# Window attention scores as one full-array product a tile, and routing selections over 128 rows, in a one-core transformer-and-Mamba kernel

## The chip, the cores and the metric

The kernel runs on one NeuronCore of a Trainium2 chip. The metric is the device time of one execution in microseconds (us). Engines are named as the profile names them: PE is TensorE (PEld its weight loads), DVE is VectorE, ACT is ScalarE, POOL is GpSimd, SP is SyncE, which here only issues DMAs. The profile gives the clock that was granted to TensorE as a share: 1.00 is 2.4 GHz, 0.50 is 1.2 GHz.

## The reference

The input is 4 images of 64 x 64 tokens with 64 channels. Three blocks follow one another:

```
xw = windows of 8 x 8 tokens; q, k, v = split(xw @ qkv_w.T + qkv_b), 8 heads of 8
q, k = rope2(q), rope2(k)
attn = softmax(q * hd**-0.5 @ k.T);  h = (attn @ v) @ proj_w.T + proj_b
...
h = h + mamba(layernorm(h))          # 128 inner channels, 16 states, a scan over 4096 tokens
...
logits = softmax(relu(f @ router_w1 + b1) @ router_w2 + b2)     # f = layernorm(h), 6 experts
top_w, top_i = top_k(logits, 2);  weights = softmax(top_w)
out = sum over the two chosen experts of weight * expert(f)     # three layers each
h = h + out
```

## The kernel before

The 16384 tokens are cut into 16 chunks of 1024 (16 image rows, so 16 attention windows). The stages are laid over one another: while chunk c is scanned, chunk c+1 is prepared (convolution, silu, softplus), c+2 is projected and normalised, c+3 is attended, and c-1 goes through router and experts. A round of the program (`body(c, odd)`, c from -3 to 17) has 32 slots, written out by hand: each engine has its own program with the same slots, and in each slot it does in a fixed order what falls due there. Engines run in order and are tied by semaphores. Score tiles belong to slots 18 to 25 of round c (`attention_at`, line 285, gives chunk c+3 and s = n - 9 from slot 9 on, and the rest of its steps in slots 0 to 8 of the next round).

**Scan.** For each slot, SP spreads rows of delta and x*delta from DRAM over 128 partitions (8 channels by 16 states), ACT makes the decay (L776), DVE multiplies by the spread B (L1015, "feed") and scans 512 tokens (L1024), POOL multiplies the result by the spread C (L1273), and PE collects four such products at every fourth slot (L439). ACT makes the decay of slot n+2 only after the scan of slot n. The B of a half chunk is spread by PE with L429: that for the first half of the next chunk in slot 30. POOL's product of slot n has to be there before DVE scans slot n+4.

**Attention.** Eight pairs of windows make a chunk. A tile w is one pair: 128 queries (64 of the upper window, 64 of the lower) against 8 heads by 64 keys. `q_diag` holds the queries of tile w as 128 x 128 with two filled quarters: the 64 channels of either window stand in their own 64 partitions and give 64 of the 128 output rows; the other two quarters are zero, from the setup on. For odd tiles the two halves of the output are swapped. `k_heads` holds the keys, zero outside the head's 8 channels. `scores` (L521) makes the scores of two tiles at once: two products of 64 rows by 64 columns for each, in the four quarters of the array, each over 512 columns, into banks 4 and 5 (a use's `fill` waits until the bank's use before was drained). They are only there for the maxima: DVE reduces each tile (L1044) to the negative maximum of every query and head, one tile a slot in slots 19 to 26. The eight results are transposed (L472), and `turned` makes the scores again in transposed form (L544), with the maxima added (L546), ACT takes the exponential (L795), and L559 multiplies by the values.

**Experts.** The routing weights of chunk c-1 (6 experts, a high and a low part in fp32r, for two groups of tokens: 24 rows) are computed by DVE in slots 15 to 19, transposed by PE in slot 22 (L646) into `wT`, and `weights` (L665) makes six products with `w_sel` in slots 23 to 28 (L673), each of which copies a weight over 64 output rows. One bank serves all six: each waits for ACT's copy of the one before (in slots 24 to 29). POOL multiplies the expert's second layer by it (L1345, slots 25 to 30) and `layer3` (L709; L714 in the profile) adds it up in slots 27, 29 and 31. The bias products L653 stand in slot 25. The first and second expert layers are L694 and L705 (slots 15 to 20), with ACT's activations L956 and L960.

PE's order within a slot is: B spread, first attention steps, late expert steps, y collection, C spread, expert steps, preparation, attention (score tiles among it), projection, expert layers, selections.

```
725    k, s = attention_at(c, n)
...
736    if has(c) and n % 4 == 1 and n >= 5:
737        collect(c, odd, (n - 5) // 4)
...
744    if has(k):
745        attend(k, s)
...
749        layers(c - 1, n, before_layers)
750        weights(c - 1, n, *before_weights)
```

Of the kernel before, what the change touches and what calls it, by code (L numbers as in the profile page):

```python
# [7 lines left out]
F32 = mybir.dt.float32  # L8
F32R = mybir.dt.float32r
# [12 lines left out]
NW = IMG // WIN  # L22
# [3 lines left out]
E, EP, RH = 6, 3, 32  # L26
# [38 lines left out]
for _w in range(NW):  # L65
# [17 lines left out]

AT = {"S": [9, 11, 13, 15], "max": [10 + _w for _w in range(NW)],
      "T": [19, 20, 22, 23, 25, 26, 28, 29], "P": [21, 21, 24, 24, 27, 27, 30, 30]}
# [30 lines left out]
def tower(nc, x, packed, select, out):  # L116
    with ExitStack() as ctx:
        def sb(name, shape, dt=F32):
            return ctx.enter_context(nc.sbuf_tensor(name, shape, dt))
# [17 lines left out]
        A = bank_uses("a", A_USES, 4)  # L137
# [10 lines left out]
        wts = sb("wts", [128, N_KEPT])  # L148
        w_sel = sb("w_sel", [4 * E, 2 * EP, 128], F32R)
        eps = sb("eps", [128, 6])  # L150
# [11 lines left out]
        q_diag = sb("q_diag", [128, NW, 128])  # L162
# [38 lines left out]
        fT = sb("fT", [128, 512])  # L201
        wT = sb("wT", [4 * E, 512], F32R)
        eb3_2 = sb("eb3_2", [4 * E, 2, C])
# [13 lines left out]
        def col(name, a=0, b=None):  # L217
            lo, hi = COL[name]
            lo2, hi2 = lo + a, hi if b is None else lo + b
            if lo >= N_KEPT:  # L220
                return once[:, lo2 - N_KEPT:hi2 - N_KEPT]
            return wts[:, lo2:hi2]
# [197 lines left out]
        def _(pe):  # L420
# [22 lines left out]
            def fill(use, k):  # L443
                if use.index or past(k - 1):
                    pe.wait_ge(use.drained, use.opens(k))
# [28 lines left out]
            def attend(k, s):  # L474
# [18 lines left out]
                if s in AT["S"]:  # L493
                    scores(k, 2 * AT["S"].index(s))
                for w in range(NW):
# [25 lines left out]
            def scores(k, w):  # L521

                uses = A[f"S{w}"], A[f"S{w + 1}"]
                for use in uses:
                    fill(use, k)
                if w == 0:
                    pe.wait_ge(heads_in.sem, heads_in.at(k, 192))
                    pe.wait_ge(heads_act.sem, heads_act.at(k, HEADS // 2))
                for odd, use in enumerate(uses):
                    for half in range(2):  # L530
                        p, to = slice(64 * half, 64 * half + 64), 64 * (half ^ odd)
                        last = pe.matmul(use.bank[to:to + 64, :], q_diag[p, w + odd, to:to + 64], k_heads[p, w + odd, :, :],  # L532
                                         start=True, stop=True)
                    last.then_inc(use.filled, 1)

# [74 lines left out]
            def experts(k, n):  # L610
# [38 lines left out]
                if n == 25:  # L649
                    use = F["outT"]  # L650
                    fill(use, k)
                    for s in range(2):
                        pe.matmul(use.bank[64 * s:64 * s + 64, :], eb3_2[:, s, :], wT[:, :].bitcast(F32),  # L653
                                  start=True, stop=True)
# [102 lines left out]
            pe.wait_ge(placed, 192)  # L757
            pe.wait_ge(setup_dve, 10)
            pe.wait_ge(setup_pool, 14)
# [4 lines left out]
        def _(act):  # L764
# [3 lines left out]
            def copy(out_, in_):  # L768
                return act.activation(out_, in_, ACT.Copy)  # L769
# [141 lines left out]
            def experts(k, n):  # L911
# [27 lines left out]
                if n == 22:  # L939
                    use = F["wT"]  # L940
                    act.wait_ge(use.filled, use.full(k))
                    copy(wT[:, :], use.bank[0:4 * E, :]).then_inc(use.drained, 1)
                if n == SLOTS:
# [60 lines left out]
            act.wait_ge(setup_pool, 14)  # L1004
            act.wait_ge(setup_dve, 10)
            rounds(body)

        @block.vector
        def _(dve):
# [181 lines left out]
            def body(c, odd):  # L1191
# [30 lines left out]
            dve.wait_ge(staged, 64)  # L1222
            dve.tensor_copy(w_sel[:, :, :], staging[0:4 * E, 0:2 * EP * 128].rearrange("p (a b) -> p a b", a=2 * EP))\
               .then_inc(setup_dve, 1)
            dve.tensor_copy(d_col[:, :], col("d_skip")).then_inc(setup_dve, 1)
            dve.tensor_scalar(conv_w[:, 0, :], col("conv_in"), col("normw"), None, ALU.mult).then_inc(setup_dve, 1)
            dve.tensor_scalar(z_w[:, :], col("z_in"), col("normw"), None, ALU.mult).then_inc(setup_dve, 1)
            dve.wait_ge(setup_dve, 6)
            dve.tensor_tensor(conv_w[:, 1, :], conv_w[:, 0, :], col("conv_tap", 128, 256), ALU.mult)\
               .then_inc(setup_dve, 1)  # L1230
            dve.wait_ge(setup_dve, 8)
            dve.tensor_tensor(conv_w[:, 0, :], conv_w[:, 0, :], col("conv_tap", 0, 128), ALU.mult)\
               .then_inc(setup_dve, 1)
            dve.wait_ge(setup_pe, 1)
            dve.tensor_copy(h_bias[:, :], b_ps[:, 0:C]).then_inc(setup_dve, 1)
            dve.wait_ge(setup_dve, 10)
            dve.wait_ge(setup_pool, 14)
# [3 lines left out]
        def _(pool):  # L1241
# [118 lines left out]

            pool.memset(staging[0:4 * E, :], 0.0).then_inc(setup_pool, 1)
            pool.memset(q_diag[:, :, :], 0.0).then_inc(setup_pool, 1)
# [11 lines left out]
            pool.wait_ge(setup_pool, 14)  # L1374
            pool.wait_ge(setup_dve, 10)
            rounds(body)
# [102 lines left out]
```

## Time and profile before

| | |
|---|---|
| time, three runs | 1921.57, 1922.06 (median), 1926.98 us |
| profiled execution | 1921.26 us |
| its span, first to last instruction | 1919.4 us |
| busy share of PE, DVE, POOL, ACT | 71%, 71%, 63%, 54% |
| mean granted TensorE clock | 0.74 |
| PE matmul records | 8212 |

An f32 matmul leaves two records in the profile, an fp32r one leaves one. A row of the profile names an instruction by its line, engine, operation and the tiles (out<-in); "64*64" behind it is the part of the array used, in rows and columns; in brackets is the idle time of the engine ahead of it and what ended it. Where rows are merged, "x8" counts the records. Records of products that share the array overlap, so a group's length is from its first start to its last end.

### The profile page before, as it was taken

The numbers are of one execution on the slowest core, as the hardware profiler recorded it, in microseconds if no ns is written. First come the engines' busy times: TensorE is split into PE (matmuls) and PEld (weight loads), VectorE is DVE, ScalarE is ACT, GpSimd is POOL, SyncE is SP. The second block draws the span as 40 slices with busy tenths as digits, with TensorE's granted clock in tenths as the row PEclk, the third lists the DMA queues.
The fourth block names the chain that finished last, engine by engine and source line by source line (L and its number), as shares of the span: only waits on it lengthen the run. The fifth ranks groups of instructions, "written<-read, shape, count | busy, mean of one in ns | idle before, by whom it ended". The sixth has DMA issues, their size and how long they took to land. (4 is left out here: it accounts for less than half of the span.)

```text
span 1919.4 us, 26560 instructions
## 1 busy us (share of the span) xinstructions
PE 1368.6 (71%) x8212; PEld 612.8 (32%) x8212; DVE 1353.5 (71%) x1834; ACT 1035.8 (54%) x1909; POOL 1207.9 (63%) x1666
## 2 busy tenths in 40 slices
PE   3675676776869687786968777685968777666565
PEld 1443242241515233141524324151524324121111
DVE  1114697778687877778697777868687777878941
ACT  2244556465655657465665646565655646554432
POOL 2205676667576766757676676757676675877651
PEclk9877777786877677686868778687867768576755
DMA  2005595657566564755666565765666575677820
GB/s 63 15 1 148 143 266 140 188 149 201 165 162 192 154 179 139 207 166 167 178 174 181 139 195 151 202 166 163 197 157 176 143 199 169 196 195 205 221 73 6
DMA packets 215205, 303.80 MB, mean 158 GB/s; under 512 B 79436, under 2 KB 79640, under 8 KB 214936
## 3 DMA queue, kind: packets, MB, share of 16 engines
q1 hardware_dynamic: 215064, 302.10, 57.1%
q8 instruction: 67, 1.10, 0.2%
q14 instruction: 74, 0.61, 0.1%
HBM read 274.75 MB, written 20.97 MB: 154 GB/s over the span
## 5 line engine op out<-in xcount | busy, mean ns | idle before, releaser
L1273 POOL TENSOR_TENSOR hc<-hs,c_rep 128x512 f32<-128x512 f32 x512 | 649.7, 1269 | 406.7 <-DVE hs L1024 406.4
L1024 DVE TENSOR_TENSOR_SCAN hs<-bank,state,xd 128x512 f32<-128x512 f32 x512 | 651.7, 1275 | 55.7 <-issue 49.3
L776 ACT ACTIVATE bank<-dl,a_neg 128x512 f32<-128x512 f32 x512 | 351.0, 687 | 371.7 <-DVE hs L1024 363.1
L1015 DVE TENSOR_TENSOR xd<-xd,bank 128x512 f32<-128x512 f32 x512 | 337.0, 663 | 101.1 <-PE bank L429 100.9
L544 PE MATMUL bank<-q_diag,k_heads 128*128 128x128 f32 x1024 | 206.1, 327 | 6.4 <-ACT top_row L769 4.9
L439 PE MATMUL bank<-hc,wts 128*32 128x512 f32 x1024 | 199.9, 843 | 5.9 <-POOL hc L1273 5.4
L544 PEld LDWEIGHTS bank<-q_diag,k_heads 128*128 128x128 f32 x1024 | 174.8, 212 | 73.3 <-issue 63.5
L705 PE MATMUL bank<-e,wts 64*64 64x512 f32 x384 | 84.2, 960 | 129.9 <-ACT e L956 129.9
L532 PE MATMUL bank<-k_heads,q_diag 64*64 64x512 f32 x512 | 92.2, 797 | 102.7 <-DVE neg_max L1044 70.6
L1044 DVE TENSOR_REDUCE neg_max<-bank 128x8 f32<-128x512 f32 x128 | 86.9, 687 | 103.8 <-PE bank L532 103.3
L1345 POOL TENSOR_TENSOR ew<-ew,e 128x512 f32<-128x512 f32 x96 | 121.0, 1261 | 33.5 <-ACT e L769 33.5
L1289 POOL TENSOR_TENSOR att<-pv,rec 128x512 f32<-128x512 f32 x16 | 17.2, 1074 | 191.5 <-DVE rec L1064 191.5
L602 PE MATMUL bank<-xz,wts 128*128 128x512 f32 x128 | 98.5, 862 | 46.9 <-ACT xz L870 41.8
L795 ACT ACTIVATE probsT<-bank 128x512 f32<-128x512 f32 x128 | 76.3, 596 | 100.1 <-PE bank L546 98.4
L1064 DVE RECIPROCAL rec<-pv 128x64 f32<-128x64 f32 x16 | 8.9, 554 | 158.7 <-ACT pv L769 158.7
L546 PE MATMUL bank<-top_row,top_sel 128*128 128x128 bf16 x512 | 119.3, 233 | 0.0
L694 PE MATMUL bank<-fT,wts 64*128 64x512 f32 x192 | 83.9, 962 | 49.1 <-ACT ew L960 46.1
L673 PE MATMUL bank<-wT,w_sel 24*128 24x512 f32 x96 | 70.8, 737 | 36.9 <-ACT e L769 33.9
L769 ACT ACTIVATE e<-bank 128x512 f32<-128x512 f32 x96 | 56.5, 589 | 52.3 <-PE bank L673 49.0
L714 PE MATMUL bank<-ew,wts 128*64 128x512 f32 x96 | 78.3, 912 | 3.8 <-POOL ew L1345 3.7
L559 PEld LDWEIGHTS bank<-v_diag,probsT 128*64 128x64 f32 x2048 | 67.3, 138 | 42.6 <-issue 36.3
L559 PE MATMUL bank<-v_diag,probsT 128*64 128x18 f32 x2048 | 75.3, 213 | 4.7 <-ACT probsT L795 4.7
(171 smaller groups left out, 2416.2 us busy)
## 6 DMA issues: line engine op xcount, KB each, us to landing
xd<-xdel_rows SPq DMA_DIRECT2D x512, 256.0 KB, 4.0
dl<-delta_rows SPq DMA_DIRECT2D x512, 256.0 KB, 3.7
delta_rows<-delta SPq DMA_DIRECT2D x16, 512.0 KB, 7.3
xdel_rows<-xdel SPq DMA_DIRECT2D x16, 512.0 KB, 4.0
xin<-in_x_dram SPq DMA_DIRECT2D x32, 128.0 KB, 2.5
q_diag<-rot SPq DMA_DIRECT2D x64, 64.0 KB
out_dram<-res SPq DMA_DIRECT2D x256, 16.0 KB
k_heads<-rot SPq DMA_DIRECT2D x128, 16.0 KB
```

Source lines behind the costliest of these rows:

```text
L439: last = pe.matmul(y_ps[32 * g:32 * g + 32, :], col("y_sel", 32 * i, 32 * i + 32), hc[:, n % 8, :], start=False, stop=True, skip_group_che ...
L532: last = pe.matmul(use.bank[to:to + 64, :], q_diag[p, w + odd, to:to + 64], k_heads[p, w + odd, :, :], start=True, stop=True)
L544: pe.matmul(use.bank[:, at], k_heads[:, w, 2 * hp:2 * hp + 2, :], q_diag[:, w, :], start=True, stop=True)
L546: last = pe.matmul(use.bank[:, at], top_sel[:, row:row + 2, :], top_row[:, :], start=False, stop=True, skip_group_check=True)
L559: last = pe.matmul(use.bank[64 * par:64 * par + 64, 18 * hp:18 * hp + 18], probsT[:, w % 2, 128 * hp + 64 * (par ^ w % 2):128 * hp + 64 * ...
L602: pe.matmul(use.bank[:, :], col(wt), xz[:, q, h, :], start=True, stop=True).then_inc(use.filled, 1)
L776: act.activation(decay_ps[n % 2][:, :], dl[:, n % 4, :], ACT.Exp, scale=a_neg[:, g:g + 1])\
L1015: dve.tensor_tensor(xd[:, n % 8, :], xd[:, n % 8, :], b_ps[:, :], ALU.mult).then_inc(injected.sem, 1)
L1024: dve.tensor_tensor_scan(hs[:, n % 4, :], decay_ps[n % 2][:, :], xd[:, n % 8, :], state[:, g:g + 1], ALU.mult, ALU.add).then_inc(scanned.s ...
L1044: dve.tensor_reduce(neg_max[:, w, :], use.bank[:, :].rearrange("p (h j) -> p h j", h=HEADS), X_AXIS, ALU.max, negate=True).then_inc(use.dr ...
L1273: pool.tensor_tensor(hc[:, n % 8, :], hs[:, n % 4, :], c_rep[:, BAND * h:BAND * h + BAND], ALU.mult)\
L1345: pool.tensor_tensor(ew[:, j, :], ew[:, j, :], wb[:, i % 2, :], ALU.mult).then_inc(weighed.sem, 1)
```

## The change

The score products are made tile by tile: `scores` makes one product of 128 x 128 over 512 columns for one tile, with the zero quarters of `q_diag` in it, and each of the eight tiles has a slot of its own (18 to 25 of the round) in place of two tiles in every other slot. The banks and the maxima's slots stay; tile w now waits for the bank's drain by tile w-2 only when its own slot comes. The selections L673 read `w_sel` and `wT` over all 128 rows: 24 filled ones and 104 of zeros, for which the staging tile and `wT` are cleared in the setup. One DVE operation is added there, and the counts of `setup_dve` that are waited for go up by one.

```diff
-AT = {"S": [9, 11, 13, 15], "max": [10 + _w for _w in range(NW)],
+AT = {"S": [9 + _w for _w in range(NW)], "max": [10 + _w for _w in range(NW)],
...
-        w_sel = sb("w_sel", [4 * E, 2 * EP, 128], F32R)
+        w_sel = sb("w_sel", [128, 2 * EP, 128], F32R)
...
-        wT = sb("wT", [4 * E, 512], F32R)
+        wT = sb("wT", [128, 512], F32R)
...
                 if s in AT["S"]:
-                    scores(k, 2 * AT["S"].index(s))
+                    scores(k, AT["S"].index(s))
...
             def scores(k, w):
 
-                uses = A[f"S{w}"], A[f"S{w + 1}"]
-                for use in uses:
-                    fill(use, k)
+                use = A[f"S{w}"]
+                fill(use, k)
                 if w == 0:
                     pe.wait_ge(heads_in.sem, heads_in.at(k, 192))
                     pe.wait_ge(heads_act.sem, heads_act.at(k, HEADS // 2))
-                for odd, use in enumerate(uses):
-                    for half in range(2):
-                        p, to = slice(64 * half, 64 * half + 64), 64 * (half ^ odd)
-                        last = pe.matmul(use.bank[to:to + 64, :], q_diag[p, w + odd, to:to + 64], k_heads[p, w + odd, :, :],
-                                         start=True, stop=True)
-                    last.then_inc(use.filled, 1)
+                pe.matmul(use.bank[:, :], q_diag[:, w, :], k_heads[:, w, :, :], start=True, stop=True)\
+                  .then_inc(use.filled, 1)
...
-                        pe.matmul(use.bank[64 * s:64 * s + 64, :], eb3_2[:, s, :], wT[:, :].bitcast(F32),
+                        pe.matmul(use.bank[64 * s:64 * s + 64, :], eb3_2[:, s, :], wT[0:4 * E, :].bitcast(F32),
                                   start=True, stop=True)
...
-                    copy(wT[:, :], use.bank[0:4 * E, :]).then_inc(use.drained, 1)
+                    copy(wT[0:4 * E, :], use.bank[0:4 * E, :]).then_inc(use.drained, 1)
...
-            dve.tensor_copy(w_sel[:, :, :], staging[0:4 * E, 0:2 * EP * 128].rearrange("p (a b) -> p a b", a=2 * EP))\
+            dve.tensor_copy(w_sel[:, :, :], staging[:, 0:2 * EP * 128].rearrange("p (a b) -> p a b", a=2 * EP))\
                .then_inc(setup_dve, 1)
+            dve.memset(wT[:, :].bitcast(F32), 0.0).then_inc(setup_dve, 1)
...
-            pool.memset(staging[0:4 * E, :], 0.0).then_inc(setup_pool, 1)
+            pool.memset(staging[:, :], 0.0).then_inc(setup_pool, 1)
```

## Rows read from the trace of the kernel before

**Rows 1.** The page: busy us of PE, its share of the span, its instructions.

```profile
PE 1368.6 (71%) x8212; PEld 612.8 (32%) x8212; DVE 1353.5 (71%) x1834; ACT 1035.8 (54%) x1909; POOL 1207.9 (63%) x1666
```

**Rows 2.** Stretches: us; busy us (instructions) of PE, PEld, DVE, ACT, POOL; clock, DMA, GB/s.

```profile
1037.50:1146.80 109.30, 83.06 (x515) 37.70 (x513) 84.74 (x115) 64.04 (x119) 75.06 (x103) 0.75 0.63 172
1108.48:1118.72 10.24, 6.39 (x29) 1.28 (x28) 8.47 (x13) 5.39 (x11) 5.85 (x11) 0.50 0.82 224
1125.54:1142.61 17.07, 15.40 (x46) 5.09 (x46) 12.75 (x15) 8.29 (x15) 16.11 (x20) 0.50 0.70 212
1142.61:1173.33 30.72, 28.26 (x288) 19.08 (x284) 20.73 (x25) 20.93 (x40) 16.97 (x24) 1.00 0.70 187
```

**Rows 3.** Waits of the whole span: us in total, times, longest us.

```profile
DVE neg_max L1044 <- PE bank L532: 103.3, 40, 13.4
...
PE bank L532 <- DVE neg_max L1044: 70.6, 34, 3.8
```

**Rows 4.** Timeline, DVE: start us, us, instruction, count, idle before and what ended it.

```profile
1112.61 0.69 DVE L1044 TENSOR_REDUCE neg_max<-bank 128x8 f32<-128x512 f32 x1 [0.39 <-PE bank L532]
...
1120.92 0.69 DVE L1044 TENSOR_REDUCE neg_max<-bank 128x8 f32<-128x512 f32 x1 [3.49 <-PE bank L532]
...
1145.61 1.29 DVE L1015 TENSOR_TENSOR xd<-xd,bank 128x512 f32<-128x512 f32 x2 [6.77 <-PE bank L429]
```

**Rows 5.** Timeline of PE, slots 20 to 22 of that chunk.

```profile
1110.60 1.99 PE L532 MATMUL bank<-k_heads,q_diag 64*64 64x512 f32 x8 [2.07 <-DVE neg_max L1044]
1114.36 1.99 PE L705 MATMUL bank<-e,wts 64*64 64x512 f32 x8 [1.78 <-ACT e L956]
1116.28 1.94 PE L439 MATMUL bank<-hc,wts 128*32 128x512 f32 x8
1118.14 0.87 PE L646 MATMUL bank<-wts,w_parts 128*24 128x128 f32 x4
1118.85 1.02 PE L602 MATMUL bank<-xz,wts 128*128 128x512 f32 x2
1119.80 1.09 PE L532 MATMUL bank<-k_heads,q_diag 64*64 64x512 f32 x8
```

**Rows 6.** Timeline of PE, slots 25 to 31 of that chunk.

```profile
1129.12 1.97 PE L653 MATMUL bank<-wT,eb 24*64 24x512 f32 x4
...
1136.19 0.80 PE L544 MATMUL bank<-q_diag,k_heads 128*128 128x128 f32 x2
...
1138.94 0.79 PE L673 MATMUL bank<-wT,w_sel 24*128 24x512 f32 x1
1139.66 1.94 PE L439 MATMUL bank<-hc,wts 128*32 128x512 f32 x8
1141.53 1.12 PE L714 MATMUL bank<-ew,wts 128*64 128x512 f32 x1
...
1143.05 0.49 PE L544 MATMUL bank<-q_diag,k_heads 128*128 128x128 f32 x2
...
1144.43 1.08 PE L429 MATMUL bank<-xz,wts 128*128 128x512 f32 x2
...
1146.39 0.62 PE L714 MATMUL bank<-ew,wts 128*64 128x512 f32 x1
```

**Rows 7.** Timeline of POOL, the fourth and the sixth expert product.

```profile
1136.78 1.25 POOL L1345 TENSOR_TENSOR ew<-ew,e 128x512 f32<-128x512 f32 x1
...
1141.97 1.25 POOL L1345 TENSOR_TENSOR ew<-ew,e 128x512 f32<-128x512 f32 x1
```

**Rows 8.** Timeline of PE in the next chunk, a full product at the low clock.

```profile
1182.36 1.71 PE L602 MATMUL bank<-xz,wts 128*128 128x512 f32 x2
```

**Rows 9.** Timeline, the first score phase, ahead of the first scan.

```profile
38.51 1.98 PE L532 MATMUL bank<-k_heads,q_diag 64*64 64x512 f32 x8 [9.32 <-DMA q_diag<-rot]
...
41.95 1.99 PE L532 MATMUL bank<-k_heads,q_diag 64*64 64x512 f32 x8 [1.46 <-DVE neg_max L1044]
...
50.85 1.29 DVE L1044 TENSOR_REDUCE neg_max<-bank 128x8 f32<-128x512 f32 x2 [2.16 <-PE bank L532]
```

More of the change, by code:

```diff
@@ L757, in _ @@
             pe.wait_ge(placed, 192)
-            pe.wait_ge(setup_dve, 10)
+            pe.wait_ge(setup_dve, 11)
             pe.wait_ge(setup_pool, 14)
@@ L1004, in _ @@
             act.wait_ge(setup_pool, 14)
-            act.wait_ge(setup_dve, 10)
+            act.wait_ge(setup_dve, 11)
             rounds(body)
@@ L1227, in _ @@
             dve.tensor_scalar(z_w[:, :], col("z_in"), col("normw"), None, ALU.mult).then_inc(setup_dve, 1)
-            dve.wait_ge(setup_dve, 6)
+            dve.wait_ge(setup_dve, 7)
             dve.tensor_tensor(conv_w[:, 1, :], conv_w[:, 0, :], col("conv_tap", 128, 256), ALU.mult)\
                .then_inc(setup_dve, 1)
-            dve.wait_ge(setup_dve, 8)
+            dve.wait_ge(setup_dve, 9)
             dve.tensor_tensor(conv_w[:, 0, :], conv_w[:, 0, :], col("conv_tap", 0, 128), ALU.mult)\
@@ L1235, in _ @@
             dve.tensor_copy(h_bias[:, :], b_ps[:, 0:C]).then_inc(setup_dve, 1)
-            dve.wait_ge(setup_dve, 10)
+            dve.wait_ge(setup_dve, 11)
             dve.wait_ge(setup_pool, 14)
@@ L1374, in _ @@
             pool.wait_ge(setup_pool, 14)
-            pool.wait_ge(setup_dve, 10)
+            pool.wait_ge(setup_dve, 11)
             rounds(body)
```

## The prediction

> **What bounds the kernel now.** I read the engines' shares first: no engine is full, TensorE (PE) is busy 71% of the span [rows 1]. So the end is set by work that passes from engine to engine. The stretches view of one middle chunk comes next: a chunk takes 109.3 us and PE's granted clock is 0.75 on average, because it moves between its two levels, 0.50 (1.2 GHz) and 1.00 (2.4 GHz) [rows 2]. Ten us from 1108.48 and seventeen from 1125.54 run at 1.2 GHz, thirty from 1142.61 at 2.4. In the seventeen, PE is busy 15.40 us and still has the low level; in the thirty it is busy just as densely (28.26 of 30.72) and has the high one. Busy time does not tell the two apart. What PE did does: in the first it ran selections of 24 rows and expert-bias products of 24 rows by 64 columns, with some full work between them; in the second it ran mostly the full-width transposed scores.
>
> The waits view says that vector (DVE) waited 103.3 us for score products (L532), and PE waited 70.6 us at that line for DVE's maxima to empty the banks [rows 3]. The DVE timeline shows where: 3.49 us before the fifth maximum (1120.92), 0.39 before the third, and 6.77 us at 1145.61, for the B spread (L429) of the next chunk [rows 4]. Each is PE's doing. The first is the end of a gapless run of PE that starts at 1114.36, when the activations of the h1 layer land: h2 layer, y collection, wT transposes, C spread, then the pair of score tiles that the maximum wants [rows 5]. The last is the end of a nearly gapless run from 1129 to 1145.5 [rows 6], at 1.2 GHz until 1142.61 [rows 2]. GpSimd (POOL) runs beside it without a gap, 2.6 us for each slot (a scan's product by C and an expert product), and hands over its fourth and sixth expert products at 1138.03 and 1143.22 [rows 7]. PE takes them up only at 1141.53 and 1146.39 [rows 6]: it is PE that is late, by 3.5 and 3.2 us.
>
> **The change, part by part.** Everything is set against the profiled execution, 1921.26 us with its span of 1919.4; the median of the runs shown is 1922.06, 0.8 above.
>
> *Score products cost twice the array time.* A pair of tiles is now four products that share the array, 1.99 us at 1.2 GHz and 1.09 at 2.4 [rows 5]. A full 128 x 128 product over 512 columns is 1.71 us at 1.2 GHz [rows 8] and 1.02 at 2.4 [rows 5], and two are needed: +1.4 or +0.95 us a pair. Eight tiles in place of four pairs are +4 to +6 us of PE work a chunk. Where it falls decides.
>
> *Score products are spread, one a slot.* Tile w now waits for the maximum of tile w-2, not w-1. Tiles 0 to 2 and 5, 6 stand where PE waits anyway (the gap at 1110.60 was 2.07 us [rows 5]; 34 such gaps ended with a maximum [rows 3]): I cost them at nothing; if that cover were gone, at 1 to 1.7 us each. The 0.39 before the third maximum goes too, but what ends the h2 wait at 1114.36 is the scan of slot 20, which is not earlier, so nothing is gained by it.
>
> *Tile 3 comes into the first gapless run*, behind the collection of slot 21, at 1118.14. Clock 1.2 GHz until 1118.72, so a third of its 1.71 us there and two thirds at 1.02: 1.25 us. Tile 4 alone in place of the pair is 0.07 less. So the fifth maximum is **1.1 to 1.2 us later** and pushes DVE and POOL behind it. Bounds: 1.7 later if all is at 1.2 GHz; if the run were at 2.4 from its start, the 1.99 + 1.94 of h2 layer and collection would be about 1.0 each, and it would come 0.8 earlier.
>
> *Tile 7 comes into the second run*, between the collection of slot 25 and the bias products at 1129.12: 1.02 or 1.71 us.
>
> *The selections.* Six products a chunk (0.79 us at 1.2 GHz) load 128 rows in place of 24. The moving columns are the same 512, so I cost them at nothing in themselves; the bounds are 0 and, if they took as long as a full f32 product, 0.9 each. What I expect of them is the clock. From slot 22 on PE now has five score tiles of full width and six full-height selections where it had two pairs and six 24-row ones. That is the kind of work it did before the clock rose at 1142.61 and while it stayed high. I expect the high level, granted at 1118.72, to last through, or to come back within a few us of 1129.
>
> *What that gives.* At 2.4 GHz the bias products (1.97), the selections (0.79), tile T0 (2.75 from start to start, 1.38 for T1 at the high level) and the collection (1.94 against about 1.05) shrink by more than half of the 15 us [rows 6], and PE is then held by POOL, which is 1.1 later: fourth expert product 1138.03 + 1.1 = 1139.1, layer 3 1.0, T1 1.4, so the B spread starts at 1141.5, not 1144.43, 2.9 us earlier. The third layer-3 product waits for 1143.22 + 1.1 = 1144.3, not 1146.39: **2.1 us earlier**, and PE is gapless from there through the transposed scores, so this is what is carried on. Twelve chunks have scores, experts and selections together: 12 x 2.1 = 25 us.
>
> *The first three score phases* (before the scans start) are a plain alternation: 1.98 us pair, two maxima, next pair 3.44 us after the last, 13.6 us in all [rows 9]. With one tile a product, PE runs on while DVE reduces. At 1.2 GHz throughout that is 8 x 1.71 + 0.7 = 14.4, 0.8 worse; with the clock rising after about three tiles it is 3 x 1.71 + 5 x 1.02 + 0.7 = 10.9, 2.7 better, and the two transposed tiles behind it gain 1.4 each at the high level. The third phase has some of the high level already. I take 4 + 4 + 2 = 10 us.
>
> *Setup.* One more memset on DVE (512 columns, about 0.5 us); the two operations on more partitions have the same columns. 0.5 us.
>
> Sum: 25 + 10 - 0.5 = 34 to 35 us of 1921.3: **1887 us**.
>
> The Trainium skill (TensorE: Matmul & The Clock Gate, What's actually happening) says that the gate sets the clock by how busy PE has recently been. Taken as time busy, padding would change nothing and the sum would be that of the first rival. The trace does not agree: 15.40 busy us of 17.07 at 1.2 GHz.
>
> **The rivals.**
>
> *Slower: the clock stays as it is.* The width of the products may not be what it follows, or the added work may come just outside the stretches that count. Then tile 3 (1.2) and tile 7 (1.7) lie on the two gapless runs and nothing is returned: 2.9 us for 12 chunks, 35, and the first phases +2: 1958. For it: both runs are gapless [rows 5, 6]. Against: the two stretches of rows 2. It decides as soon as less than 2.9 us a chunk come back between 1125 and 1146. The Trainium skill (TensorEngine Tiling, Theoretical Speedup) speaks for this side: halving a small dimension gives up to 2x, and the change gives that up. The trace agrees, with 1.09 us for a packed pair and 1.02 for one full product.
>
> *Larger gain.* The high level also covers the first run (1114.36 on). The fifth maximum is then 0.8 earlier, not 1.1 later, so POOL too, and layer 3 comes 2.1 + 1.9 = 4 us earlier: 12 x 4 + 12 = 60, 1861. Against: PE waits 2.07 + 1.78 us ahead of 1114.36 for other engines [rows 5], and the change leaves it little else to do there. For: tiles 0 to 2 add full work ahead of it.
>
> *Given back.* The gain moves all that follows forward against the clock's steps. The low level at the h2 layers may last longer for it, or a chunk may settle on the same clock pattern of 109.3 us, and 2 us a chunk are lost again; only the start gains: 1911.
>
> *Nothing.* If PE's lateness in both runs had other cover, or gain and cost cancel, 1920.
>
> **How the numbers follow.** Main case 0.40, larger gain 0.18, given back 0.12, nothing 0.08, slower 0.22. Faster is the first three, 0.70; same 0.08; slower 0.22. Likeliest: 1887. The main case's own range is 1872 to 1902 (1 us a chunk either way). The range of all reaches from beyond the larger gain, 1845, to 1940, half way into the slower case (its price halved where one of the two tiles finds cover). About 0.3% (6 us) is what a measurement of this kernel can tell from no change.
>
> **What would show it.** Score products should be 256 records of 128 x 128, about 0.5 to 0.9 us each. DVE's wait for them should fall from 103 us to about half, with the one before the fifth maximum growing, not shrinking. The stretch that answers to 1125 to 1142 should have a granted clock above 0.75, and DVE's wait for L429 should be 3 to 4 us a chunk in place of 6.8. The selections should keep their time at each level. The mean clock should rise from 0.74 to 0.80 or more. The prediction is wrong if that stretch stays at 0.5, if the selections get longer, or if a chunk outside of it grows by as much as is gained in it.

## The result, and the profile after

The change makes the kernel **slower**, by 1.2%: 1945.90 us (median of four runs, 1944.89 to 1948.84) against 1921.82 (four runs, 1921.21 to 1926.98), a ratio of 1.0122 with a 95% interval of 1.0101 to 1.0143. Forecast were 1887 and a range of 1845 to 1940. The profiled execution took 1946.53 us, with a span of 1944.7 and a mean granted clock of 0.758 (before: 1919.4 and 0.740).

The page's shares after (the columns as in [rows 1]):

```profile
PE 1379.2 (71%) x7956; PEld 634.7 (33%) x7956; DVE 1347.7 (69%) x1835; ACT 1036.5 (53%) x1909; POOL 1209.5 (62%) x1666
```

256 PE records fewer, and 10.6 us more busy time. The groups of the two edited lines, by form (busy us, mean ns, idle before), behind the one of the score products before:

```profile
L532 PE MATMUL bank<-k_heads,q_diag 64*64 64x512 f32 x512 | 92.2, 797 | 102.7 <-DVE neg_max L1044 70.6 <-DMA q_diag<-rot 32.1
...
L528 PE MATMUL bank<-k_heads,q_diag 128*128 128x512 f32 x256 | 164.5, 751 | 32.0 <-DMA q_diag<-rot 29.3 <-issue 2.1 <-DVE neg_max L1039 0.6
...
L668 PE MATMUL bank<-wT,w_sel 128*128 128x512 f32 x96 | 73.1, 762 | 91.2 <-ACT e L764 79.0 <-ACT c_rep L764 10.7 <-ACT wT L764 1.5
```

PE works 72 us longer at the scores, 4.5 us a chunk, where 4 to 6 were forecast. Its wait for DVE's maxima has gone, but for a rest: it was 70.6 us in [rows 3] and 24.1 more ahead of the weight loads, and is 0.6 and 12.8 now. But the waits of the span show what DVE paid for that (us in total, times, longest):

```profile
DVE neg_max L1039 <- PE bank L528: 166.1, 50, 13.3
...
DVE xd L1010 <- PE bank L429: 65.9, 18, 4.7
```

DVE waits 63 us more for score products than in [rows 3]. For the B spread it waits 35 us less than before, where that row stood at 100.9. Now one middle chunk, the tenth ([rows 2] is the ninth), and three stretches, of which the last reaches into the next chunk (columns of [rows 2]):

```profile
1157.40:1270.10 112.70, 85.10 (x499) 39.35 (x497) 84.70 (x116) 64.12 (x120) 75.15 (x104) 0.74 0.60 167
1229.30:1239.50 10.20, 5.99 (x19) 1.04 (x18) 5.64 (x10) 4.80 (x10) 4.86 (x10) 0.50 0.57 173
1246.40:1263.40 17.00, 11.96 (x30) 4.11 (x31) 11.99 (x15) 6.97 (x12) 10.69 (x14) 0.50 0.59 163
1263.40:1297.60 34.20, 31.05 (x304) 20.28 (x304) 22.27 (x27) 23.45 (x44) 22.77 (x30) 1.00 0.72 196
```

The chunk takes 112.7 us in place of 109.3. PE is at 1.2 GHz for seventeen us near the end of the chunk, as before, but is busy for only 12 of them, where [rows 2] had 15.4: it now waits there itself. DVE's timeline in this chunk (start, us, idle before and what ended it) says when DVE waits; these are its only waits in slots 19 to 31, and [rows 4] are the ones they answer to:

```profile
1240.21 0.69 DVE L1039 TENSOR_REDUCE neg_max<-bank 128x8 f32<-128x512 f32 x1 [5.16 <-PE bank L528]
...
1254.79 0.69 DVE L1039 TENSOR_REDUCE neg_max<-bank 128x8 f32<-128x512 f32 x1 [5.00 <-PE bank L528]
...
1268.88 1.28 DVE L1010 TENSOR_TENSOR xd<-xd,bank 128x512 f32<-128x512 f32 x2 [3.95 <-PE bank L429]
```

The first is before the fourth maximum (slot 22), the second before the eighth (slot 26). The wait of 3.49 before the fifth is gone, and the one for the B spread went from 6.77 to 3.95. The waits shown here add up to 14.1 us, those of [rows 4] to 10.7: that is about the 3.4 us by which the chunk is longer. POOL stands still with DVE ahead of slot 25's product:

```profile
1256.75 1.27 POOL L1269 TENSOR_TENSOR hc<-hs,c_rep 128x512 f32<-128x512 f32 x1 [4.83 <-DVE hs L1019]
```

PE's timeline tells why both new ones are there; it answers to [rows 5, 6]:

```profile
1234.82 1.99 PE L700 MATMUL bank<-e,wts 64*64 64x512 f32 x8 [4.21 <-ACT e L951]
1236.73 1.94 PE L439 MATMUL bank<-hc,wts 128*32 128x512 f32 x8
1238.60 1.57 PE L528 MATMUL bank<-k_heads,q_diag 128*128 128x512 f32 x2
...
1248.19 0.79 PE L668 MATMUL bank<-wT,w_sel 128*128 128x512 f32 x1 [2.90 <-ACT e L764]
1248.91 1.94 PE L439 MATMUL bank<-hc,wts 128*32 128x512 f32 x8
1250.78 1.97 PE L648 MATMUL bank<-wT,eb 24*64 24x512 f32 x4
1252.68 2.08 PE L528 MATMUL bank<-k_heads,q_diag 128*128 128x512 f32 x2
1253.76 1.42 PE L668 MATMUL bank<-wT,w_sel 128*128 128x512 f32 x1
```

Tile 3 (1238.60, slot 21) comes behind the h2 layer, for which PE waits 4.21 us, and behind the collection. Tile 7 (1252.68, slot 25) comes behind a selection that waits 2.90 us for ACT, a collection and the bias products. Each tile is wanted by a maximum in the very next slot. PE works in order, so DVE waits out the whole queue ahead of the tile. Before, both were made in pairs with the tile ahead of them, two slots before their maximum.

**The account.** The first scan starts at 163.8 us in place of 179.2 (-15.4). From there to the first scan of the fourteenth chunk 1444.2 us pass in place of 1404.5 (+39.7). The rest takes 336.7 in place of 335.7 (+1.0). The sum is +25.3, the difference of the spans.

The start is a plain gain. The timeline of the first score phase, against [rows 9]:

```profile
38.38 9.21 PE L528 MATMUL bank<-k_heads,q_diag 128*128 128x512 f32 x16 [9.16 <-DMA q_diag<-rot]
...
40.46 0.69 DVE L1039 TENSOR_REDUCE neg_max<-bank 128x8 f32<-128x512 f32 x1 [13.28 <-PE bank L528]
...
47.62 0.69 DVE L1039 TENSOR_REDUCE neg_max<-bank 128x8 f32<-128x512 f32 x1 [0.36 <-PE bank L528]
```

The eight maxima end at 48.3, and ended at 52.1 before.

### The profile page after: what moved, and what is told of

It reads as the page before. It is cut to its first block and busy times, and to the rows that moved or that the text cites. A ratio compares the mean times of both kernels' runs of the same rounds, so it can differ in the third digit from the quotient of the medians.

```text
span 1944.7 us, 25985 instructions
## 1 busy us (share of the span) xinstructions
PE 1379.2 (71%) x7956; PEld 634.7 (33%) x7956; DVE 1347.7 (69%) x1835; ACT 1036.5 (53%) x1909; POOL 1209.5 (62%) x1666
## 5 line engine op out<-in xcount | busy, mean ns | idle before, releaser
L539 PE MATMUL bank<-q_diag,k_heads 128*128 128x128 f32 x1024 | 194.6, 314 | 6.4 <-ACT top_row L764 4.9
L439 PE MATMUL bank<-hc,wts 128*32 128x512 f32 x1024 | 185.9, 782 | 9.0 <-POOL hc L1269 4.5
L539 PEld LDWEIGHTS bank<-q_diag,k_heads 128*128 128x128 f32 x1024 | 169.7, 204 | 61.8 <-issue 52.1
L528 PE MATMUL bank<-k_heads,q_diag 128*128 128x512 f32 x256 | 164.5, 751 | 32.0 <-DMA q_diag<-rot 29.3
L668 PE MATMUL bank<-wT,w_sel 128*128 128x512 f32 x96 | 73.1, 762 | 91.2 <-ACT e L764 79.0
L597 PE MATMUL bank<-xz,wts 128*128 128x512 f32 x128 | 94.6, 830 | 47.4 <-ACT xz L865 41.8
L689 PE MATMUL bank<-fT,wts 64*128 64x512 f32 x192 | 76.1, 876 | 36.8 <-ACT ew L955 33.8
L528 PEld LDWEIGHTS bank<-k_heads,q_diag 128*128 128x128 f32 x256 | 50.3, 226 | 137.7 <-issue 124.3
L700 PEld LDWEIGHTS bank<-e,wts 64*64 64x64 f32 x384 | 14.9, 183 | 217.9 <-ACT e L951 217.9
L668 PEld LDWEIGHTS bank<-wT,w_sel 128*128 128x128 f32 x96 | 24.9, 259 | 170.7 <-ACT e L764 108.0
```

The source lines that it names most:

```text
L439: last = pe.matmul(y_ps[32 * g:32 * g + 32, :], col("y_sel", 32 * i, 32 * i + 32), hc[:, n % 8, :], start=False, stop=True, skip_group_che ...
L528: pe.matmul(use.bank[:, :], q_diag[:, w, :], k_heads[:, w, :, :], start=True, stop=True)\
L539: pe.matmul(use.bank[:, at], k_heads[:, w, 2 * hp:2 * hp + 2, :], q_diag[:, w, :], start=True, stop=True)
L597: pe.matmul(use.bank[:, :], col(wt), xz[:, q, h, :], start=True, stop=True).then_inc(use.filled, 1)
L668: pe.matmul(use.bank[:, :], w_sel[:, j, :], wT[:, :], start=True, stop=True)\
L700: last = pe.matmul(use.bank[to:to + 64, :], col("ew2", at, at + 64)[p], e1[p, s, :], start=True, stop=True)
```

## The experiments

"Chunk time" is the distance between the first scans of two neighbouring middle chunks in the timeline; the idle times named are DVE's in a middle chunk that corresponds to the one above. The slots of the score tiles are those of `AT["S"]` plus 9. Where that list gives two tiles the same slot, `attend` goes through all tiles of the slot:

```diff
-                if s in AT["S"]:
-                    scores(k, AT["S"].index(s))
+                for w in range(NW):
+                    if s == AT["S"][w]:
+                        scores(k, w)
```

### One part of the change alone

**Only the spreading** (e2): the kernel after, with the tiles in quarters of the array again, one tile a slot, and the selections over 24 rows.

```diff
-                pe.matmul(use.bank[:, :], q_diag[:, w, :], k_heads[:, w, :, :], start=True, stop=True)\
-                  .then_inc(use.filled, 1)
+                for half in range(2):
+                    p, to = slice(64 * half, 64 * half + 64), 64 * (half ^ w % 2)
+                    last = pe.matmul(use.bank[to:to + 64, :], q_diag[p, w, to:to + 64], k_heads[p, w, :, :],
+                                     start=True, stop=True)
+                last.then_inc(use.filled, 1)
...
-                    pe.matmul(use.bank[:, :], w_sel[:, j, :], wT[:, :], start=True, stop=True)\
+                    pe.matmul(use.bank[:, :], w_sel[:, j, :], wT[0:4 * E, :], start=True, stop=True)\
```

> The changed kernel's slots (one tile a slot), but each tile as two products in two array quarters as before, and the selections over 24 rows. Theory A: both 5 us waits are there, since they come from the place and not from the product; with no clock gained 1945 to 1970. Theory B: the cost was the full product, so about 1922. At the start of the kernel a tile alone takes as long as a pair did (1.99 us), so 2 to 3 us more in each of the three score phases.

1989.41 us, ratio 1.0357 (1.0339 to 1.0374). The chunk time is 116.1, the first scan starts at 167.2. Its waits:

```profile
DVE neg_max L1042 <- PE bank L530: 170.8, 38, 13.2
DVE xd L1013 <- PE bank L429: 107.8, 17, 7.8
```

The two new waits are there with products in quarters too (5.2 us before the fourth maximum, 4.9 before the eighth), and so are 12 of the 15.4 us that the start gains. But this run is not free of the added array time. A tile that is made alone in quarters keeps PE about as long as a pair did: 1.97 us at 1.2 GHz, against 1.99 in [rows 5]. Its score products and those of the next run (e3), by form:

```profile
1283.12 1.97 PE L530 MATMUL bank<-k_heads,q_diag 64*64 64x512 f32 x4
...
L530 PE MATMUL bank<-k_heads,q_diag 64*64 64x512 f32 x512 | 146.1, 782 | 37.2 <-DMA q_diag<-rot 29.3 <-DVE neg_max L1042 5.7 <-issue 2.1
...
L530 PE MATMUL bank<-k_heads,q_diag 128*128 128x512 f32 x256 | 174.7, 820 | 82.1 <-DVE neg_max L1041 50.0 <-DMA q_diag<-rot 32.1
```

So e2 alone does not tell the place of the tiles from their array time. The next run does.

**Only the full-array products** (e3): the kernel before, still two tiles in every other slot.

```diff
-                    for half in range(2):
-                        p, to = slice(64 * half, 64 * half + 64), 64 * (half ^ odd)
-                        last = pe.matmul(use.bank[to:to + 64, :], q_diag[p, w + odd, to:to + 64], k_heads[p, w + odd, :, :],
-                                         start=True, stop=True)
-                    last.then_inc(use.filled, 1)
+                    pe.matmul(use.bank[:, :], q_diag[:, w + odd, :], k_heads[:, w + odd, :, :],
+                              start=True, stop=True).then_inc(use.filled, 1)
```

> The kernel before with its pairs in slots 18, 20, 22, 24, but each tile one full 128 x 128 product; selections as before. Theory A: no wait of 5 us; about 1 us more ahead of the fifth maximum, returned where the clock is higher: 1900 to 1935. Theory B: 1940 to 1950, as the changed kernel has.

1912.99 us, ratio 0.9963 (0.9950 to 0.9976). The first scan starts at 172.9, which is 6.3 of the 8.3 us by which the span is shorter, and the chunk time stays at 109.3. PE spends 174.7 us on the scores here, more than the 164.5 of the kernel after, and neither of the 5 us waits is there. The added array time in the old slots costs nothing, so the loss is that of the place. This is also the run that has the packing given up and nothing else: it is not slower for it.

**Only the selections over 128 rows** (e4): the kernel before, with the change's edits to `w_sel`, `wT` and the setup, and nothing of `scores` or `AT`.

> The kernel before, with the selections over 128 rows and nothing else. Theory A: a selection keeps its 0.79 us at 1.2 GHz, the clock in the stretch of the selections rises earlier, 1895 to 1922, in no case slower than before by over 3 us. Theory B says nothing of it. Theory C: either exactly a chunk of 109.2 us again (1922) or one shorter by a whole step of the clock's pattern, some 3.4 us, for twelve chunks (1881).

1891.08 us against 1921.10, ratio 0.9846 (0.9832 to 0.9861): **30.0 us faster**. The first scan is where it was (179.2). Of the chunk times, twelve lie between 105.4 and 108.8, and the wait for the B spread falls to 3.5 us a chunk:

```profile
DVE neg_max L1044 <- PE bank L532: 101.6, 40, 13.4
...
DVE xd L1015 <- PE bank L429: 64.1, 18, 6.4
```

The first row is that of [rows 3] within 2 us: only the second changed, from 100.9.

**The change without that part** (e5): the kernel after, selections over 24 rows.

```diff
-                    pe.matmul(use.bank[:, :], w_sel[:, j, :], wT[:, :], start=True, stop=True)\
+                    pe.matmul(use.bank[:, :], w_sel[:, j, :], wT[0:4 * E, :], start=True, stop=True)\
```

> The changed kernel with the selections over 24 rows as before, all else as changed. If the selections' rows raise the clock (as they did alone: 1891 against 1921), this is 25 to 40 us slower than the changed kernel, 1970 to 1985. If the gain was used up by the wait before the eighth maximum, the two are the same within 6 us.

1988.45 us, ratio 1.0334 (1.0293 to 1.0374), chunk time 116.1, 7.4 us of wait for the B spread. That is the time of e2 (whose run of before was at 1921.10, this one's at 1922.66), so with the tiles spread their full width is worth nothing (a lone tile takes nearly as long in quarters). The padded selections are worth 2.1% in the changed kernel (1.0334 against 1.0122), more than the 1.5% of e4. **The parts:** spreading alone +3.6%, padding alone -1.5%, full width alone -0.4%, together +1.7% where the change has +1.2%. The difference is about the 0.6% by which padding is worth more once the tiles are spread. The spreading is the only part that costs, and it costs more than the other two give.

### The two late tiles

**Tile 3 in slot 20** (e6) and **tile 7 in slot 24** (e7), each beside the tile ahead of it, alone:

```diff
-AT = {"S": [9 + _w for _w in range(NW)], "max": [10 + _w for _w in range(NW)],
+AT = {"S": [9, 10, 11, 11, 13, 14, 15, 16], "max": [10 + _w for _w in range(NW)],
```

> The changed kernel with tile 3 alone moved back, to slot 20; tile 7 stays in slot 25. Theory A: DVE's wait of 5.2 us before the fourth maximum goes, one of 3.4 before the fifth comes in its place (4.1 to 5 us of 12 chunks cannot be gained, 1 to 2 can), that of 5.0 before the eighth stays: 1920 to 1938. Theory C: a chunk of 112.6 or of 109.2 us and nothing between, 1946 or 1905.

```diff
-AT = {"S": [9 + _w for _w in range(NW)], "max": [10 + _w for _w in range(NW)],
+AT = {"S": [9, 10, 11, 12, 13, 14, 15, 15], "max": [10 + _w for _w in range(NW)],
```

> The changed kernel with tile 7 alone moved back, to slot 24; tile 3 stays in slot 21. Theory A: the 5.0 us before the eighth maximum go whole, nothing takes their place, and this is the larger of the two: 1885 to 1905, 3.4 us or more a chunk below the changed kernel. Theory C: 109.2 or 105.8 us a chunk, 1905 or 1864.

e6: 1940.45 us, ratio 1.0082 (1.0056 to 1.0109), chunk time 112.6 as in the kernel after. Its DVE timeline, the two waits for score products in a middle chunk:

```profile
1237.81 0.69 DVE L1040 TENSOR_REDUCE neg_max<-bank 128x8 f32<-128x512 f32 x1 [4.20 <-PE bank L529]
...
1250.02 0.69 DVE L1040 TENSOR_REDUCE neg_max<-bank 128x8 f32<-128x512 f32 x1 [5.01 <-PE bank L529]
```

The wait has moved from the fourth maximum to the fifth, which is in the place of [rows 4]: tile 4 now stands behind the same h2 layer. Of the 1.0 us by which this wait is shorter than the 5.16 before, the wait for the B spread takes back 0.7 (4.62 us), and the chunk time stays. That tile 4 stands in the way is not the whole of it: with tile 7 moved too (e1 below), the same move of tile 3 is worth 38 us.

e7: 1901.88 us, ratio 0.9882 (0.9843 to 0.9921), chunk time 109.2. Of its timeline, the only two waits of DVE in slots 21 to 31:

```profile
1212.16 0.69 DVE L1040 TENSOR_REDUCE neg_max<-bank 128x8 f32<-128x512 f32 x1 [5.44 <-PE bank L529]
...
1236.73 1.29 DVE L1011 TENSOR_TENSOR xd<-xd,bank 128x512 f32<-128x512 f32 x2 [4.92 <-PE bank L429]
```

**This one tile decides the sign:** made a slot earlier, it is worth 44 us (1945.9 to 1901.9), with the same products, and the changed kernel is then 21 us faster than the one before (1922.66 beside it).

**Both** (e1):

```diff
-AT = {"S": [9 + _w for _w in range(NW)], "max": [10 + _w for _w in range(NW)],
+AT = {"S": [9, 10, 11, 11, 13, 14, 15, 15], "max": [10 + _w for _w in range(NW)],
```

> The changed kernel, with the score tiles in slots 18, 19, 20, 20, 22, 23, 24, 24 in place of one a slot: tile 3 stands ahead of the h2 layer again and tile 7 ahead of the second selection. Theory A (lost lead: tiles 3 and 7 come only one slot ahead of their maxima, behind a run of PE that waits for ACT): DVE's two waits of 5 us a chunk for a score tile go, the 15 us gained before the first scan stay, a chunk takes 109.3 us or less, the time is 1880 to 1908. Theory B (the array time of full products is the cost): the same products are made, so the time stays near 1946. Theory C (a chunk settles on a pattern of the clock's steps, whatever the waits): 33 steps remain or 32 come, the time jumps to about 1906 or stays at 1946, and nothing between.

1864.01 us, ratio 0.9706 (0.9691 to 0.9721), chunk time 105.8: 38 us below e7, by tile 3 alone, with tile 4 still behind the h2 layer. The time is below all that was expected of it (1880 to 1908). In its DVE timeline one maximum still waits, the fifth:

```profile
1188.56 0.69 DVE L1040 TENSOR_REDUCE neg_max<-bank 128x8 f32<-128x512 f32 x1 [3.42 <-PE bank L529]
```

### The fifth maximum, which waited in the kernel before too

**Tile 4 in slot 21** (e8), and **in slot 20 with tile 3** (e9), ahead of the h2 layer; tile 5 a slot earlier in both:

```diff
+AT = {"S": [9, 10, 11, 11, 12, 13, 15, 15], "max": [10 + _w for _w in range(NW)],
```

> Slots 18, 19, 20, 20, 21, 22, 24, 24: as the run with tiles 3 and 7 early (1864 us), and tile 4 before the wT transposes and the C spread in place of behind them. Theory A: the fifth maximum's wait falls from 3.4 to about 1.5 to 2 us, 2 us for twelve chunks: 1840 to 1850. Theory C: no change at all (1864, a chunk of 105.8) or a chunk of 102.4 (1823).

```diff
+AT = {"S": [9, 10, 11, 11, 11, 13, 15, 15], "max": [10 + _w for _w in range(NW)],
```

> Slots 18, 19, 20, 20, 20, 22, 24, 24: tile 4 too ahead of the h2 layer, right after the third maximum. Theory A: DVE's last wait for a tile, 2.9 to 3.4 us before the fifth maximum, goes; the h2 layer starts 0.5 to 1 us later, 2 us a chunk are left, 1835 to 1845. Theory C: 105.8 (1860) or 102.4 us a chunk (1820).

e8: 1859.88 us, ratio 0.9662 (0.9616 to 0.9708), chunk time 105.8, and 2.9 us of wait before the fifth maximum. In slot 21 the tile is still behind the h2 layer. e9: **1826.09 us**, ratio 0.9500 (0.9476 to 0.9524), chunk time 102.4, and no maximum waits in a middle chunk. In slot 20 the tile needs the bank that DVE's third maximum empties. PE's timeline there:

```profile
1155.42 1.13 PE L529 MATMUL bank<-k_heads,q_diag 128*128 128x512 f32 x2 [0.49 <-DVE neg_max L1040]
1156.91 1.09 PE L701 MATMUL bank<-e,wts 64*64 64x512 f32 x8 [0.36 <-ACT e L952]
```

The tile lies in the time in which PE would wait for the h1 activations anyway: the h2 layer behind it waits only 0.36 us, where it waited 1.78 in [rows 5] and 4.21 in the kernel after. Both rows are also at 2.4 GHz (1.09 against 1.99 us for the same layer).

**The bias products a slot earlier too** (e12, on top of e8):

```diff
-                if n == 25:
+                if n == 24:
```

> The run with tile 4 sooner (1860 us), with the bias products (L653 of the kernel before, 2.0 us at 1.2 GHz) moved from slot 25 to slot 24, where PE waits for a maximum. Theory A: the late run of PE is 1 to 2 us shorter, the B spread comes as much earlier, 1840 to 1850. Theory C: 1860 or 1820.

1858.23 us, ratio 0.9671 (0.9650 to 0.9692), chunk time 105.8: nothing over e8. There these products stand behind all score tiles. Whether their place costs nothing or a step of the chunk time (below) hides it, this run does not tell.

### Does a chunk's time only move in steps?

The chunk times so far were 102.4, 105.8, 109.2, 112.6 and 116.1, each 3.4 or 3.5 from the next. **Two maxima made twice** (1.2 us of DVE a chunk, the second result unused), in e1 (e10) and in the kernel before (e11):

```diff
+                    if w in (0, 1) and has(k - 3):
+                        dve.tensor_reduce(spare[:, w, :], use.bank[:, :].rearrange("p (h j) -> p h j", h=HEADS),
+                                          X_AXIS, ALU.max, negate=True)
```

> The run with tiles 3 and 7 early (1864 us, 105.8 us a chunk), with the maxima of tiles 0 and 1 made a second time, into a spare tile, in thirteen chunks: 0.6 us each, 1.2 a chunk, on a stretch in which DVE has no gap and PE's h2 layer waits for it in the end. Theory A alone (waits add up): 12 or 13 times 1.2 us more, 1879. Theory C (a chunk settles on the clock's pattern): 105.8 us a chunk again, 1861 to 1868, the 1.2 us taken from the waits behind; or 109.2 and 1905.

> The same two doubled maxima in the kernel before (109.2 us a chunk). Theory A alone: 1.2 us a chunk more, 1937. Theory C: 109.2 us a chunk again and 1919 to 1926, or 112.6 and 1966.

e11: 1925.82 us, ratio 1.0033 (1.0014 to 1.0051), chunk time unchanged at 109.2. The waits for score products fell from 103.3 to 95.1 us and took up about half of the 15 us of added work. e10: 1885.29 us, ratio 0.9814 (0.9793 to 0.9834), 21.3 above e1 and so more than the work added, with chunk times mostly of 107.3 to 107.8. So a chunk often settles on one of these times and absorbs a small cost, but it need not: e10 and e4 lie between them.

The expectations had two theories for this. Where only the waits were added up (theory A), the time was missed by 8 to 19 us in e1, e2, e8, e9, e11 and e12: the chunk moved by 0, 3.4 or 6.8 us instead. Where a chunk could only move by such steps (theory C), e6 to e9, e11 and e12 came within 7 us, and e1, e4 and e10 did not. So the runs show which wait goes when a tile is moved, but not why a chunk gives 3.4 us or nothing for it. What holds a chunk at a step is left open.

### Width of the tiles and of the selections, without the late tiles

The slots of e9, with the tiles in quarters and selections over 24 rows (e13), full tiles and 24 rows (e14), and quarters and 128 rows (e15). The edits are those of e9, e2 and e5.

> Slots 18, 19, 20, 20, 20, 22, 24, 24, but each tile as two products in two array quarters, and the selections over 24 rows: the place of the tiles alone. If place is all (theory A) it gives 1835 or less; if the fast version needs what full width and 128 rows did to the clock, the late run is at 1.2 GHz as in the kernel before and the B spread is 3 us late again: 1865 to 1885.

> The same slots, full 128 x 128 products, selections over 24 rows. If the selections' rows are what raises the clock late in a chunk, 3.4 us a chunk more than the fastest version (1826), 1865 to 1870; if the width of the tiles is, 1826 again.

> The same slots, tiles in quarters, selections over 128 rows. If full width is worth nothing but its array time, this is as fast as 1826 or faster; if full width helps the clock, 1835 to 1865, with the start of the scans 3 us later (167 against 164).

| tiles | selections | us | ratio (95%) | chunk time |
|---|---|---|---|---|
| quarters (e13) | 24 rows | 1863.82 | 0.9691 (0.9660 to 0.9723) | 105.8 |
| full (e14) | 24 rows | 1863.65 | 0.9696 (0.9663 to 0.9729) | 105.8 |
| quarters (e15) | 128 rows | 1823.50 | 0.9491 (0.9452 to 0.9530) | 102.4 |
| full (e9) | 128 rows | 1826.09 | 0.9500 (0.9476 to 0.9524) | 102.4 |

Whether a tile is one full product or two in quarters makes no difference, but this does not compare it with a packed pair: a tile alone is nearly as long in quarters (e2). The rows of the selections make 38 to 40 us. Stretches of a middle chunk and of its last part, from 88 us into it, for e13, e15 and e9 (columns of [rows 2]):

```profile
1101.80:1207.60 105.80, 83.97 (x515) 38.22 (x513) 84.47 (x115) 64.20 (x120) 75.00 (x103) 0.77 0.61 178
1189.80:1207.60 17.80, 15.47 (x81) 7.11 (x83) 10.24 (x12) 7.97 (x15) 15.48 (x18) 0.62 0.62 183
```

```profile
1074.20:1176.60 102.40, 79.99 (x515) 37.19 (x515) 84.62 (x116) 64.04 (x120) 75.07 (x104) 0.82 0.65 184
1162.20:1176.60 14.40, 11.27 (x83) 6.02 (x81) 10.50 (x13) 7.97 (x15) 14.40 (x18) 0.88 0.80 230
```

```profile
1079.40:1181.80 102.40, 80.50 (x497) 38.19 (x497) 84.56 (x116) 64.04 (x119) 75.03 (x104) 0.82 0.63 184
1167.40:1181.80 14.40, 11.27 (x81) 6.01 (x79) 10.49 (x13) 7.97 (x15) 14.40 (x18) 0.88 0.75 229
```

The stretch is 3.4 us shorter at a granted clock of 0.88 in place of 0.62, and POOL is busy through all of it (14.40 of 14.40), where in e13 it stands still for 2.3 us. The wait that ends sooner is the B spread's, in the waits of e13 and of e15:

```profile
DVE xd L1014 <- PE bank L429: 108.3, 17, 7.7
```

```profile
DVE xd L1014 <- PE bank L429: 63.2, 18, 4.7
```

## Why the prediction was wrong

**What failed is the step "Tile 7 comes into the second run", costed as 1.02 or 1.71 us on PE.** Two things are wrong in it. The place: it was put between the collection of slot 25 and the bias products, but the expert steps come ahead of attention in PE's order, so it stands behind the bias products. And its consumer was not followed: the eighth maximum wants the tile one slot later, and DVE stands still for 5.00 us and POOL for 4.83 until it comes. For tile 3 such a wait was traced, for tile 7 it was not. Slot 25 of DVE went from 2.4 to 7.5 us. e7 takes this wait away and gets 3.4 us a chunk and 44 us in all, more than the whole distance from the kernel before to the one after. Its 1901.9 lies inside the range that was stated.

**Tile 3: about right in size, wrong in place.** "1.1 to 1.2 us later" for the fifth maximum was the forecast. DVE's slots 21 and 22 together took 8.3 to 8.6 us (ninth to eleventh chunk) and take 10.0 or 10.1. But the wait is before the fourth maximum (5.16), which wants tile 3, and none is left before the fifth. Both hang on the same h2 layer, so the sum is nearly the same. What the tile costs in the end was not a matter of this size: its return to slot 20 gives 5.5 us with tile 7 late (e6) and 38 with tile 7 early (e7 to e1).

**The selections: right in themselves, and alone (e4) in their gain too.** They take 0.79 us at 1.2 GHz (1248.19 above), as in [rows 6]. The one behind tile 7 is recorded with 1.42, but it starts 1.0 us before that tile's product ends and ends 0.4 us behind it. e4 has this part alone, and gains 30.0 us where 25 were forecast for the clock. But it was put down to five full score tiles and six full-height selections together, and e13 to e15 show that the full width of the tiles adds nothing to it.

**In the changed kernel the forecast rise of the clock did not come.** The stretch that was to be above 0.75 is at 0.50, for 17.0 us (1246.40 above) as before, and the prediction had named this as a sign of being wrong. DVE's wait for the B spread was forecast at 3 to 4 us and is 3.95, but not because that stretch is faster than before. The last 24.7 us of the chunk before, in the kernel after, and in e5, which has 24 rows and the same two waits of 5 us:

```profile
1122.10:1146.80 24.70, 20.68 (x102) 8.04 (x104) 17.38 (x21) 10.87 (x20) 19.80 (x24) 0.65 0.56 171
```

```profile
1245.40:1270.10 24.70, 18.62 (x96) 7.90 (x98) 15.75 (x20) 10.34 (x19) 17.95 (x23) 0.65 0.65 178
```

```profile
1275.60:1300.30 24.70, 21.87 (x96) 8.42 (x97) 12.30 (x15) 9.22 (x17) 17.03 (x20) 0.57 0.55 149
```

With the late tiles and 24 rows the clock is lower than before (0.57), and the 128 rows bring it back to 0.65. Against e5 they do what was said of them: the wait for the B spread falls from 7.4 to 3.95 us. The same length of e9's chunk, with tiles 3, 4 and 7 early, has 0.93:

```profile
1157.10:1181.80 24.70, 20.21 (x121) 8.47 (x116) 20.80 (x27) 14.73 (x28) 22.59 (x32) 0.93 0.78 228
```

With tile 7 alone early (e7) it is 0.79. So the clock's gain over the kernel before was lost to the late tiles too.

The Trainium skill (TensorE: Matmul & The Clock Gate, What's actually happening) lets the clock follow how busy PE has recently been. These runs do not agree, if that is taken as time: e13 is busy 15.47 of 17.80 us (87%) at 0.62, and e9 11.27 of 14.40 (78%) at 0.88.

**The start: right in direction, too small.** 10 us were forecast and 15.4 measured. The forecast's own working gives 5.5 us a phase (2.7 for the tiles and 1.4 for each of two transposed ones), of which 4 was taken. It all hung on the clock, and that came: the transposed products right behind the maxima take 0.44 us in the kernel after (49.53) and 0.74 before (53.80). e3, in pairs and so without more overlap of PE and DVE, gains 6.3 us; e2, with quarters, gains 12.0; both have 0.44 there too. How much of the 15.4 is overlap (PE makes the next tile while DVE reduces) and how much is clock was not separated.

**The rivals.** "Slower" named the right side, and its price (35 us for 12 chunks) is close to the +39.7 measured between the first scans. Its condition came true as well, since the stretch stays at 0.50. But the loss is not the PE time of the two tiles (1.2 and 1.7 us) that it priced: e3 has such array time and loses nothing. It is the wait of DVE for tile 7, which no case contained, so the likeness of the two numbers is luck. Its converse argument, that the packed pair does the work in half the time, did not decide anything either. The Trainium skill (TensorEngine Tiling, Theoretical Speedup) gives up to 2x for packing; the durations agree (1.09 us a pair and 1.02 for one full product [rows 5]), yet e3, which gives the packing up in the old slots, is 0.4% faster than the kernel before. "Given back" was right that chunk times tend to settle (112.6 is one of five that recur), but not in its number, 1911.

**What would have shown it.** Of the marks that were set, the 256 records, the selections' time and the wait for the B spread came as said. Three did not. The stretch stayed at 0.50, and the mean clock rose to 0.758 in place of 0.80. And the wait for score products grew to 166 us where half of 103 was forecast, with the one before the fifth maximum gone and not grown: that mark alone would have pointed at the failed step.

## What to carry to other kernels

When one of two products made together is moved to a later slot, ask for every single one how many slots lie between it and its consumer, and what stands ahead of it in its own engine's order: with one slot of lead, the waits and the work of its engine ahead of it become the consumer's wait (5.00 us before the eighth maximum), and one more slot of lead for that one tile gave 44 us back (e7). Do not judge such a move by one run: the same move of tile 3 was worth 5.5 us with tile 7 late (e6) and 38 with tile 7 early (e7 to e1). A product that shares the array gains from it only beside its partner: a tile alone in quarters took 1.97 us, and a pair 1.99. Try the parts of a mixed change by themselves: here the padding was worth 30 us by itself, and with tiles 3, 4 and 7 earlier two versions are 5% below the kernel before and 6% below the one after, e9 (1826) and e15 (1824).

## What the runs showed of the hardware that was not expected

Rows of zeros sped up a kernel at no cost in instruction time. Selections over 128 rows in place of 24, with the same 512 columns and the same 0.79 us at 1.2 GHz, took 30 us (e4), 2.1% or 41 us (after against e5), 37.6 (e9 against e14) and 40.3 (e15 against e13) off, each time with more of the chunk's end at 2.4 GHz (the last 24.7 us at 0.65 in place of 0.57 in the kernel after against e5). Giving the score tiles full width did nothing of the sort: e14 has 0.62 in its last 17.9 us, like e13. Why the one helps and the other does not is open.

The chunk times came mostly as 102.4, 105.8, 109.2, 112.6 and 116.1 us, whatever was changed, and 1.2 us of added work on DVE left the 109.2 as it was. They are not the only ones (e10, e4).
